# Scores and maxima of an attention layer in pairs of 64-row products, and outputs turned in 32x32 blocks by VectorE

## What is computed

```python
qkv = layernorm(x) @ w_qkv + b_qkv                       # q, k, v: 12 heads x 1024 x 32
attn = (q * scale) @ k.T                                 # 1024 x 1024 for each head
attn = attn + rel_h[..., :, None] + rel_w[..., None, :]  # q . table of row / column distances
out = softmax(attn, axis=-1) @ v
x = x + out @ w_proj + b_proj
x = x + moe(layernorm(x))                                # top 2 of 8 experts, 384 -> 1536 -> 384
```

## Time and profile before

| | |
|---|---|
| median of three runs | 600.71 us (600.52 to 601.66) |
| profiled execution | 602.2 us, its span 600.4 us |
| granted TensorE clock, mean over the span | 0.989 of full speed |
| busy: TensorE matmuls / VectorE / ScalarE / GpSimd | 587.5 / 378.6 / 296.2 / 205.4 us |
| twelve heads | about 78 to 276 us |
| 135 to 150 us: TensorE / VectorE / ScalarE / GpSimd busy | 15.00 / 10.47 / 7.64 / 13.64 us |

### The profile page before, as it was taken

The page is one execution under the profiler, slowest core; times in us unless marked ns, Lnnn a source line. Parts: engine busy times, 40 slices in busy tenths (PEclk is TensorE's granted clock), DMA queues, the critical chain, the costliest instruction groups (busy, mean ns, idle before and its releaser), DMA issues.

```text
span 600.4 us, 11444 instructions
## 1 busy us (share of the span) xinstructions
PE 587.5 (98%) x4453; PEld 511.3 (85%) x4453; DVE 378.6 (63%) x633; ACT 296.2 (49%) x414; POOL 205.4 (34%) x122
## 2 busy tenths in 40 slices
PE   7999999999999999999999999999999999999996
PEld 6787977766677766668988999999999999999994
DVE  6646777676777776714978865554567545377523
ACT  4555245555555555563655444454545444455524
POOL 1400068889898888898021000000000000000002
PEclk9999999999999999999979999999999999999999
DMA  8046064443333344103412444543443444442302
GB/s 258 27 87 133 2 132 89 89 90 81 68 66 69 67 88 87 41 2 107 140 59 81 157 158 157 155 145 129 137 148 100 149 147 159 157 158 87 112 1 105
DMA packets 38615, 63.40 MB, mean 106 GB/s; under 512 B 3912, under 2 KB 34478, under 8 KB 38446
## 3 DMA queue, kind: packets, MB, share of 16 engines
q1 hardware_dynamic: 38574, 62.83, 37.2%
HBM read 44.16 MB, written 1.57 MB: 76 GB/s over the span
## 4 chain that ended last, share of the span: by engine, by line
PE 91%; DMA 2%; ACT 2%; DVE 1%; SPq 1%; POOL 1%; issue 1%; POOLq 0%; DVEq 0%
PE ps L869 21%; PE ps L885 21%; PE ps L641 13%; PE ps L650 9%; PE ps L545 9%; PE ps L628 7%; PE ps L577 2%; PE ps L800 1%; PE ps L588 1%; PE ps L896 1%; PE ps L812 1%; SPq L369 1%; PE ps L527 1%; PE ps L674 1%; DMA kst<-kp 1%
## 5 line engine op out<-in xcount | busy, mean ns | idle before, releaser
L1259 DVE TENSOR_REDUCE rhalf<-ps 128x1 f32<-128x512 f32 x192 | 130.9, 690 | 33.4 <-PE ps L628 33.2
L456 POOL TENSOR_TENSOR acc<-acc,prob 128x1024 f32<-128x1024 f32 x58 | 139.7, 2408 | 8.7 <-ACT prob L1042 4.0
L1042 ACT ACTIVATE prob<-ps 128x1024 f32<-128x1024 f32 x96 | 98.1, 1028 | 80.5 <-PE ps L641 80.4
L641 PE MATMUL ps<-qst,kst 128*128 128x512 f32 x384 | 115.3, 396 | 0.5 <-DMA qst<-mneg 0.3
L869 PE MATMUL ps<-xeh,wih 128*128 128x320 f32 x288 | 89.6, 311 | 1.0 <-ACT xeh L1106 1.0
L885 PE MATMUL ps<-hh,woh 128*128 128x320 f32 x288 | 89.2, 310 | 0.0
L885 PE MATMUL ps<-hh,wol 128*128 128x320 f32 x288 | 89.0, 309 | 0.0
L869 PE MATMUL ps<-xeh,wil 128*128 128x320 f32 x288 | 89.0, 309 | 0.0
L885 PE MATMUL ps<-hl,woh 128*128 128x320 f32 x288 | 89.0, 309 | 0.0
L869 PE MATMUL ps<-xel,wih 128*128 128x320 f32 x288 | 89.0, 309 | 0.0
L492 POOL CAST dpc<-dpt 120x1024 fp32r<-120x1024 f32 (+1 forms) x3 | 3.1, 1040 | 240.6 <-PE ps L905 216.5
(11 more groups left out here) (167 smaller groups left out, 889.1 us busy)
## 6 DMA issues: line engine op xcount, KB each, us to landing
raw_i<-in_L_ffn_wi SPq DMA_DIRECT2D x32, 576.0 KB, 5.2
raw_o<-in_L_ffn_wo SPq DMA_DIRECT2D x32, 576.0 KB, 4.0
xs<-in_x SPq DMA_DIRECT2D x8, 384.0 KB, 4.5
qst<-qh SPq DMA_DIRECT2D x12, 256.0 KB, 3.1
qst<-relh SPq DMA_DIRECT2D x12, 256.0 KB, 3.9
qst<-relw SPq DMA_DIRECT2D x12, 256.0 KB, 4.4
kst<-kp SPq DMA_DIRECT2D x12, 256.0 KB, 5.1
qst<-ql SPq DMA_DIRECT2D x12, 128.0 KB, 3.1
```

Of the source, the lines that this page charges most:

```text
L456: nc.gpsimd.tensor_tensor(acc[:, :], acc[:, :], prob[:, slot_of(j, t), :], ALU.add).then_inc(sum_add, 1)
L641: last = mm(bank(2 * (t % 2) + half), kst[b][:, part, t * P:(t + 1) * P], qst[b][:, part, half * BANK:(half + 1) * BANK], start=part == 0, ...
L1042: run(prob[:, slot_of(j, t), :], ps[:, 2 * (t % 2) * BANK:2 * (t % 2 + 1) * BANK], ACT.Exp).then_inc(exp_done, 1)
L1259: ve.tensor_reduce(rhalf[:, p // 2, p % 2:p % 2 + 1], bank(max_bank(b, p)), AX_X, ALU.max).then_inc(max_red, 1)
```

## The change

- **Rows.** The operands of a head become `qm` and `km`. The queries are halved: partitions 0 to 63 hold the first 512 queries, 64 to 127 the second. Each half has 32 rows of channels and 32 rows of other terms, in four forms for the queries (low part with the low part of the column term and the negated maxima; high part with the high column term; high part with the row term, twice) and two for the keys. A product now has 64 rows; `scores` makes three pairs for each key tile (first half, second half, each into its own bank), `max_scores` eight pairs a head, of the high parts only.
- **Row term.** The maxima's products no longer hold it. ScalarE keeps the table in `relhn`, and VectorE adds it while it takes the maximum: one `tensor_tensor_reduce` for each 512 keys, which writes the sum back into the bank and carries the first half's maximum into the second. `whole_max` and the half maxima go.
- **Column term.** VectorE subtracts from it one column (`rcol`, copied by ScalarE), in `rel_shift`, in place of ScalarE's copy; the tables are made in the order column, row.
- **Output.** VectorE turns bank 6 in blocks of 32x32 into `osb` and divides from there; ScalarE's copy and TensorE's transposes go. `attn` has another layout, and `turn_attn`, `attn_high`, `attn_low` follow it. Bank 6 is free after the turn.
- **Order.** Quarter products and transposes stand in four groups in a head. GpSimd adds six tiles instead of seven, TensorE sums two. VectorE divides before the thirteenth maximum, six maxima are taken a head ahead, three of their pairs for the second head behind the values. VectorE's loop over heads is written out.
- **Loads.** Twelve a head instead of six, in two groups with semaphores of their own: the maxima wait for the first, the scores for both. The constant rows come by eight loads instead of one; four fills of constant rows by GpSimd go.
- **Router stage.** For tiles 1, 4 and 5 ScalarE copies the projection and GpSimd adds it; GpSimd makes the high parts of all tiles; the projection's and the statistics' order changes; the logits' products write 64 columns (eight copies of the eight) and some filler products go; GpSimd starts its part of the dispatch masks one step earlier.

```diff
...
+    qm = [place(f"qm{b}", [P, 4, BANK], F32R, at_b) for b, at_b in enumerate((q0, q1, x0))]
+    km = [place(f"km{b}", [P, 2, T], F32R, at_b + 8 * T) for b, at_b in enumerate((q0, q1, x0))]
...
-        REL = [(kind, c, half) for c in range(DC) for kind in range(2) for half in range(2)]
+        REL = [(kind, c, half) for c in range(DC) for kind in (1, 0) for half in range(2)]
...
+        PROJ_ORDER = [0, 2, 1, 3, 4, 5, 6, 7]
         PAIRS_T = NT // 2
-        ADDED = 7
+        PV_STEPS = PAIRS_T + 1
+        ADDED = 6
...
+        R_POOLED = (1, 4, 5)
+        R_OWN = NT - len(R_POOLED)
...
+                first, rest = [], []
+                for side in range(2):
+                    low, cols = side * P // 2, slice(side * BANK, (side + 1) * BANK)
+                    own, near = slice(low, low + HD), slice(low + HD, low + 2 * HD)
+                    first += [(km[b][own, :, :], kp[rows, :, chunk, :]),
+                              (qm[b][own, HIGH:4, :], qh[rows, chunk, cols].unsqueeze(1).broadcast_to([HD, 3, BANK])),
+                              (qm[b][near, LOW:HIGH + 1, :], relw[rows, chunk, side, :, :])]
+                    rest.append((qm[b][own, LOW, :], ql[rows, chunk, cols]))
+                    for v in range(2):
+                        kh = slice(rows.start + v * HALF_ROWS, rows.start + (v + 1) * HALF_ROWS)
+                        rest.append((qm[b][near, 2 + v, :], relh[kh, :, chunk, cols]))
+                for parts, arrived in ((first, max_in[b]), (rest, rest_in[b])):
+                    for dst, src in parts:
+                        sp.dma_start(dst.bitcast(F32), src.bitcast(F32)).then_inc(arrived, 16)
...
+            for n, t in enumerate(R_POOLED):
+                pool.wait_ge(r_left, n + 1)
+                nc.gpsimd.tensor_tensor(xs[:, t, :], r_sum[:, n, :], xs[:, t, :], ALU.add).then_inc(r_pooled, 1)
+            for t in range(NT):
+                pool.wait_ge((xn_dve, xn_act)[t % 2], NT // 2 + t // 2 + 1)
+                nc.gpsimd.tensor_copy(th[:, t, :], tn[:, t, :]).then_inc(th_ready, 1)
...
-                    pe.wait_ge(heads_in[b], HEAD_IN * (n + 1))
+                    pe.wait_ge(max_in[b], MAX_IN * (n + 1))
                 if p == 2:
                     wait(pe, mneg_ready, h)
                 else:
                     wait(pe, max_red, NP * h + p - 2 + (p < 2))
-                t, half = p // 2, p % 2
-                mm(bank(max_bank(b, p)), qst[b][:, 0, t * P:(t + 1) * P], kst[b][:, 0, half * BANK:(half + 1) * BANK],
-                   start=True, stop=True).then_inc(max_mm, 1)
+                t, half, side = p // 4, p // 2 % 2, p % 2
+                rows = slice(side * P // 2, (side + 1) * P // 2)
+                mm(bank(max_bank(b, p)), qm[b][rows, HIGH, t * P:(t + 1) * P],
+                   km[b][rows, 0, half * BANK:(half + 1) * BANK], start=True, stop=True).then_inc(max_mm, 1)
 
             def turn_max(h, b):
-                pe.wait_ge(max_whole, h + 1)
+                pe.wait_ge(max_red, NP * (h + 1))
                 nc.tensor.transpose(bank(max_bank(b, NP))[0:NT, 0:P], rmax[:, :], ident[:, :]).then_inc(max_turned, 1)
 
-            def scores(h, b, t, half):
-                if half == 0:
-                    if t == 0:
+            def scores(h, n, b, t):
+                if t == 0:
+                    pe.wait_ge(rest_in[b], REST_IN * (n + 1))
+                wait(pe, exp_done, NT * h + t - 1)
+                units = [(HIGH, 0), (2 + t // HALF, 1), (LOW, 0)]
+                for k, (q_slot, k_slot) in enumerate(units):
+                    if k == 2 and t == 0:
                         pe.wait_ge(mrow_in, 16 * (h + 1))
-                    wait(pe, exp_done, NT * h + t - 1)
-                for part in range(2):
-                    last = mm(bank(2 * (t % 2) + half), kst[b][:, part, t * P:(t + 1) * P],
-                              qst[b][:, part, half * BANK:(half + 1) * BANK], start=part == 0, stop=part == 1)
-                if half == 1:
-                    last.then_inc(s_mm, 1)
+                    for side in range(2):
+                        rows = slice(side * P // 2, (side + 1) * P // 2)
+                        last = mm(bank(2 * (t % 2) + side), km[b][rows, k_slot, t * P:(t + 1) * P],
+                                  qm[b][rows, q_slot, :], start=k == 0, stop=k == 2)
+                last.then_inc(s_mm, 1)
...
+            def sum_tiles(h, b, tiles):
+                for t in tiles:
+                    pe.wait_ge(exp_done, NT * h + t + 1)
+                    quarters(slice(Q4, 2 * Q4), ones[:, 0:HD], prob[:, slot_of(b, t), :], False, False)
+            def sum_added(h, added=ADDED):
+                pe.wait_ge(sum_add, (ADDED - 1) * h + added - 1)
+                quarters(slice(Q4, 2 * Q4), ones[:, 0:HD], acc[:, :], False, True).then_inc(pv_mm, 1)
...
+                scores(h, n, b, 0)
+                if first:
+                    pe.wait_ge(v_dve, NT)
+                next_max(3)
+                if not first:
+                    values(*former, 2)
+                    values(*former, 3)
+                if last:
+                    pe.wait_ge(max_red, NP * NH)
+                    turn_attn(0)
+                scores(h, n, b, 1)
+                next_max(4)
+                scores(h, n, b, 2)
+                if not first:
+                    sum_tiles(*former, range(ADDED, NT))
+                    sum_added(h - 1)
+                next_max(5)
+                scores(h, n, b, 3)
+                next_max(6)
+                scores(h, n, b, 4)
+                next_max(7)
+                scores(h, n, b, 5)
+                if last:
+                    turn_attn(1)
+                values(h, b, 0)
+                if not last:
+                    turn_max(h + 1, (b + 1) % 3)
+                if not first:
+                    after_max(0)
+                scores(h, n, b, 6)
+                values(h, b, 1)
+                after_max(0 if first else 1)
+                scores(h, n, b, 7)
+                if first:
+                    after_max(1)
+                after_max(2)
...
-                    run(rst[:, n % 2, :], bank(n % 2), ACT.Copy).then_inc(rel_copied, 1)
+                    if kind == 1:
+                        wait(act, relw_shifted, 2 * c + half - 1)
+                        run(rcol[:, half, :], bank(n % 2).rearrange("p (g k) -> p g k", k=SIDE)[:, :, SIDE - 1],
+                            ACT.Copy).then_inc(rel_col, 1)
+                    else:
+                        run(relhn[:, c, half * HALF:(half + 1) * HALF, :].rearrange("p t k -> p (t k)"),
+                            bank(n % 2), ACT.Copy).then_inc(relh_copied, 1)
...
+            def rel_shift(n):
+                kind, c, half = REL[n]
+                if kind == 1:
+                    dve.wait_ge(rel_col, 2 * c + half + 1)
+                    wait(dve, rel_mm, n - 3)
+                    ve.tensor_tensor(rst[:, half, :].rearrange("p (g k) -> p g k", k=SIDE),
+                                     bank(n % 2).rearrange("p (g k) -> p g k", k=SIDE),
+                                     rcol[:, half, :].unsqueeze(2).broadcast_to([P, P // 8, SIDE]),
+                                     ALU.subtract).then_inc(relw_shifted, 1)
...
-                ve.tensor_reduce(rhalf[:, p // 2, p % 2:p % 2 + 1], bank(max_bank(b, p)), AX_X, ALU.max).then_inc(max_red, 1)
-            def whole_max(h):
-                dve.wait_ge(max_red, 2 * NT * (h + 1))
-                ve.tensor_reduce(rmax[:, :], rhalf[:, :, :], AX_X, ALU.max).then_inc(max_whole, 1)
+                t, half = p // 4 + HALF * (p % 2), p // 2 % 2
+                if half:
+                    dve.wait_ge(max_red, 2 * NT * h + p - 1)
+                col = h % HPG * SIDE + half * HALF_ROWS
+                here = bank(max_bank(b, p)).rearrange("p (r w) -> p r w", w=SIDE)
+                bias = relhn[:, h // HPG, t, col:col + HALF_ROWS].unsqueeze(2).broadcast_to([P, HALF_ROWS, SIDE])
+                ve.tensor_tensor_reduce(out=here, in0=here, in1=bias, scale=1.0, scalar=rpart[:, t:t + 1] if half else LOWEST,
+                                        op0=ALU.add, op1=ALU.max,
+                                        accum_out=(rmax if half else rpart)[:, t:t + 1]).then_inc(max_red, 1)
...
-                turned_o = bank(6).rearrange("p (s i j c) -> p s i j c", s=2, i=2, c=HD)
+                dve.wait_ge(pv_mm, PV_STEPS * (h + 1))
+                wait(dve, o_normed, h)
+                ve.transpose(osb[:, :], bank(6)).then_inc(o_turned, 1)
                 dve.wait_ge(o_turned, h + 1)
-                ve.reciprocal(rl[:, :, :], turned_o[:, 1, :, :, 0]).then_inc(o_rec, 1)
+                parts = osb[:, :].rearrange("p (s b d) -> p s b d", s=2, b=NT)
+                ve.reciprocal(rl[:, :], parts[:, 1, :, 0]).then_inc(o_rec, 1)
                 dve.wait_ge(o_rec, h + 1)
-                ve.tensor_tensor(attn[:, :, bass.ts(h, HD)].rearrange("p (j i) d -> p i j d", i=2),
```

(39 more changed lines are left out.)

319 lines of the change are left out of this document (142 added, 177 removed).

## The result

The changed kernel took 638.3 us (median of six runs, 635.8 to 639.8), the kernel before 600.6: 1.0625 times as long, interval 1.0603 to 1.0646. Forecast were 584 us and a range to 610. It went the other way, and beyond the rival that had the sign right (A, 607).

The account below looks back on a forecast made before the run. TensorE was taken to bound the attention stage. Ten periods -13.5, first head -1.7, last head +0.4, position terms -1.6, added pairs +1.2, router -1.5: -16.7, from 600.7 to 584 us; range 572 to 610.

Parts of the forecast that it names:

- Rival A: GpSimd's add holds out VectorE's product with two memory inputs: 17.5 us a head, kernel 607 us, chance 0.26.
- Pairs: TensorE's two 64-row products on different row halves run side by side, 0.231 us a pair, the price of one product.
- The fused instruction: VectorE's add-and-maximum, sixteen a head: 0.606 us from start to start, 0.69 long.
- the walk: One head step by step from the last quarter group of the sums, giving 15.2 us a head.
- What is late next: VectorE's stretch between sums and thirteenth maximum, in which TensorE stands still for 2.2 of a head's 15.2 us.
- The router stage: Three of eight residual sums leave VectorE, copies go to GpSimd: -1.5 us taken, bounds -3 and +1.5.
- the tie: VectorE's product at 3.27 us and GpSimd's second add at 3.28 after the sums; the product barely goes first.
- TensorE's own sum: TensorE's work alone in a head of the attention stage: 13.0 us instead of 16.5.
- the head of 15.2: Time of one head in the ten periods, 15.2 us against 16.48 before; ten periods save 13.5 us.
- The tables: Position terms before the heads: paired wide products and a removed wait, less a longer shift on VectorE, together -1.6 us.
- the values' stage: Three pairs of the second head's maxima added behind the values: +1.2 us.
- The first head: From the values to the first head's sums: 16.2 us against 17.9, so -1.7.

Follow-up runs that it names:

- r10: r2 with all six score products of a key tile on the first half of the rows, so none can run beside another: 633.4 us.
- r3: The changed kernel with 25 useless TensorE products in heads 1 to 10 before the fifteenth maximum, where TensorE only waits: 643.9 us.
- r5: The changed kernel with 13 useless TensorE products in heads 1 to 10 before the fifteenth maximum: 621.4 us, ratio 1.0344.
- r1: The changed kernel with GpSimd's second add of a head waiting until VectorE has divided the former head's outputs: 602.4 us, ratio 1.0025.
- r2: The changed kernel with reciprocal and product moved behind the six maxima taken ahead, the turn staying before the thirteenth maximum: 593.1 us, ratio 0.9866.
- r9: The changed kernel with outputs turned in place in their bank, so the product reads them there and only reciprocals from memory: 602.4 us, ratio 1.0031.
- r4: The changed kernel with VectorE's product split into eight instructions of 32 columns, each with one input tile: 700.7 us, ratio 1.1655.

## Why the prediction was wrong

**What was right.** TensorE bounded the kernel before. Pairs cost one product (r10). The fused instruction starts every 0.61 to 0.68 us, the turn takes 0.71, the unhindered product 0.42, the first add comes 0.73 and the first maximum 1.08 behind the sums (163.20 and 163.55 against 162.47), as in the walk. What is late next is indeed VectorE between the sums and the thirteenth maximum. The router stage gained 3.1, at the end of its bounds of -3 to +1.5 and twice the -1.5 taken; from which of its changes was not taken apart.

**The step that failed: the tie.** The walk put the product at 3.27 and the second add at 3.28. Measured: 3.41 and 3.20. The two fused instructions that carry the first half's maximum start 0.68 and 0.67 apart, not 0.606: 0.14 late (1.35 against 1.21). The add came 2.47 behind the first, not 2.55: 0.08 early. The text itself named 0.05 us as the point of decision. What tipped it was a step of VectorE that was slower in its loop (0.34 against 0.23), carried over to GpSimd's loop; the other way is what GpSimd's own rows of before show, in the loop and outside:

```profile
134.74 4.86 POOL L456 TENSOR_TENSOR acc<-acc,prob 128x1024 f32<-128x1024 f32 x2 [0.44 <-ACT prob L1042]
...
250.16 4.92 POOL L456 TENSOR_TENSOR acc<-acc,prob 128x1024 f32<-128x1024 f32 x2
```

Two adds took 0.06 us less in the loop, and in the changed kernel the second add comes 2.47 behind the first in it, 2.54 outside (286.25 and 288.79). A forecast that hangs on a tie of 0.01 us with both errors unknown to a tenth should have given the two sides like chances, and the side with the larger loss the wider range.

**Rival A was right in kind and 2.8 us a head too small** (17.5 against 20.3 in the middle head). Up to the thirteenth maximum it fits: product done at 5.81 (5.95 in the text), TensorE going on at 6.54. From there it had 10.7 us to the next sums; measured were 13.7. Of the 3.0 missing:
- 1.8 us is the halved clock: the same stretch took 11.94 in r3, from 171.19 to 183.37 less 0.24 for the fifteenth product that falls into it there. r5 gives 1.7 as the mean. The prediction took TensorE's speed as given, although it forecast that TensorE would stand still: this term it put at nothing without a reason.
- 0.9 us are waits for banks in front of pairs that stand too close (0.46 and 0.86 instead of 0.23 each). Rival and forecast gave 0.1 a head for that. This is the shortfall of r1 and r2, too.
- The rest, 0.3, is TensorE's own sum. The starts in r2's middle head, with every waiting pair taken at 0.23, add up to 13.9 us, not 13.0 (part of that stands before the thirteenth maximum): a pair or a group behind one of another shape starts some 0.1 late (0.80 instead of 0.70 for a tile of scores in front of quarter products), and there are about eight such switches. No run takes this part by itself.

**So was the forecast's own value.** With the clash taken away, its 584 us did not come: 602.4 (r1, r9), 593.1 (r2). It came only with the pairs spread and the adds held (580.6), which the change does not do. The gain on TensorE is real, but the head of 15.2 was 0.8 to 1.5 us too short for this order of work.

**Smaller terms.** The tables gained 0.35, not 1.6 (values begin at 62.96 instead of 63.31), and the values' stage lost 2.0, not 1.2 (17.05 instead of 15.02): a pair between the values' products costs 0.53 us there (64.46 to 65.16, less 0.17 for a product), where 0.4 was taken. The first head gained nothing of its 1.7, and the stretch from the last sums to the projection gained 1.1 where +0.4 was forecast. These were not taken apart further.

## What to carry to other kernels

Before an operand moves from a bank into memory, look at what GpSimd does at that moment: a VectorE product with both inputs in memory costs its own 0.42 us or the rest of a 2.4 us add, and who starts first decides. If it must be so, put it where nobody waits, or let the add wait for it; 0.9 us of GpSimd's time bought 3.6 a head here (r1). And a wait in front of TensorE can cost more than itself, since the clock fell in or behind it here, 1.7 us a head: fill it or price it. Where a forecast hangs on a tie, give both sides like chances.

## What the runs showed of the hardware

- TensorE's granted clock can fall behind a wait as well as in it. In the head shown it stood still from 165.7 to 169.0, worked at full speed until 170.3, then at half until 173.7, all the while busy; in four heads it fell within the wait, and in r4 (a wait of 8.33 us) at 185.6, 3.7 us before TensorE went on at half speed.
- A shorter wait is no safeguard. Waits of 1.33 to 1.48 us in r1 and r9 left the clock up in most heads, but in one head of each it fell behind a wait of 1.41: in r9 at 222.2 us, and that head took 18.4 us instead of 16.8; in r1 at 255.5.
- A maximum that is carried over from an earlier instruction costs 0.67 to 0.68 us from start to start, one that begins anew 0.61 to 0.65; each has a second record of 0.14 us that reads the result, mostly beside the next instruction.
